# Cross-attention and soft mixture of experts: a new order of the attention steps, and key and value projections as three products of fp32r parts

## The chip, the cores and the metric

The kernel runs on one core of one Trainium2 chip. The metric is the device time of one execution, in microseconds (us). The granted clock of TensorE has two levels, 1.2 and 2.4 GHz; the profile gives it as a share of the higher.

## The reference, cut to what matters

```python
# B = 16 images, N = 100 queries, S = 361 context rows, D = 256, H = 16 heads of 16
q = layernorm(x) @ wq + bq
k = ctx @ wk + bk                      # 361 x 256 per image
v = ctx @ wv + bv
alpha = softmax(q k^T / 4 + mask)      # per head, 100 x 361
x = x + (alpha v) @ wo + bo
x = x + soft_moe(layernorm(x))         # 16 experts, not touched by the change
```

All inputs are fp32, and the result is compared in fp32.

## The kernel before, in words

`attention_phase` handles the 16 images one after another in a software pipeline, then a routing phase and an expert phase follow. The change touches only the attention phase.

The pipeline has steps t = -3 to 16. In step t each engine works for five images at once: keys and queries of image t+3, values of t+2, score maxima of t+1, probabilities and their product with the values for image t, and the output projection of t-1. Steps -3, -2 and -1 fill the pipeline and have a table of their own, `AT_FILL`. Keys exist up to step 12, values up to 13, maxima up to 14, probabilities up to 15. Steps 3 to 11 are three trips of a hardware loop over three steps; the others are written out.

A step has 24 slots. `AT` says in which slot each operation stands; a number of 24 or more means the slot minus 24 of the next step. All engines run the same slots in the same order, and each engine executes its own instructions strictly in that order, so the table sets what is queued behind what. Within a slot the order is that of the code in `part`.

The operations, with their keys in the table and lines in the profile:

- rows (L715, TensorE): scores of one head pair, 100 x 362, two matmuls, into `at_rows`; VectorE then reduces them to maxima (L496). There is one such bank pair, so rows r+1 waits for the reduction of r. Eight per step.
- maxT (L837), max_parts (L546, L548, VectorE), maxrow (L250): the maxima are transposed, split and sent by four small DMAs, two on the queue of SyncE and two on that of ScalarE, into rows of `qt`. rows 0 of the next step waits for max_parts, cols 0 for the DMAs.
- cols (L737, TensorE): transposed scores, four matmuls into `at_cols`; exp (L621, ScalarE) turns them into `p_f`. cols u+1 waits for exp u. Six per step.
- pv (L757): sixteen matmuls with 32 output columns each, that is with TensorE divided into four strips. Six per step.
- v (L785) and v_copy (L612): the value projection in three pieces of 121, 121 and 119 context rows, and its copy by ScalarE. k (L771), k_hi (L632, ScalarE), k_lo (L527, VectorE): the key projection in two halves c, and its split into fp32r parts. Both write the PSUM banks `at_proj`; so k waits for the copies of v, and the reverse.
- ln (L508, L511 VectorE; L391, L393 GpSimd: the reciprocal root `rstd`), xl (L639, L644 ScalarE), xlT (L804), xlT_out (L649), q (L812), q_hi (L655), q_lo (L534): normalised queries.
- sums (L664), oT (L819), att (L515, L519), attT (L824), attT_out (L669), y (L829), x1 (L540): output.
- `next_ctx` (L283) on SyncE loads the context of image b+4 (L261) after the values of b+1 are done.

In the last steps `stay_busy` (L723) puts matmuls on unread data between the others. `hidden_scales` (L1383) works out scales for the first two experts on VectorE; it waits for a round trip of DMAs that spreads maxima over the partitions (L1367, L1370).

Keys and values are fp32 matmuls. The profile shows each of them as two matmul instructions.

Of the kernel before, what the change touches and what calls it, by code (L numbers as in the profile page):

```python
# [1978 lines left out]
```

## Time and profile before

| | us |
|---|---|
| median of 3 runs | 1083.11 (1076.62 to 1083.24) |
| profiled execution | 1084.29 |
| its span, first to last instruction | 1082.5 |
| attention phase within it | 0 to 340.3 |
| mean granted clock | 0.982 |

The span and the trace are of one profiled execution; 1.8 us of it lie outside the span. Rows of a timeline merge neighbouring instructions of one kind: start, time from the first start to the last end, and the count. A matmul's duration holds its way through the array, so the distance between starts, not the duration, tells how long it keeps TensorE.

### The profile page before, as it was taken

To read this page: it belongs to the slowest core of one execution; us is meant where nothing else is said; L and a number is where in the kernel's file an instruction comes from. 1 tells how busy PE (TensorE), PEld (TensorE's weight loads), DVE (VectorE), ACT (ScalarE), POOL (GpSimd) and SP (SyncE) were. 2 spreads that over 40 slices of the span, in tenths; PEclk is the share of its full clock that TensorE was granted. 3 is DMA by queue.
4 is the path that set the end of the run, shared out by engine and by line. 5 is a ranking of instruction groups with operands and counts; after the bars stand their busy time and mean duration, and the time that the engine had idled before them with its cause. 6 is when DMAs were issued, how large, how long until landed. Compare 5 with 4: busy or idle time off the path is not lost.

```text
span 1082.5 us, 22394 instructions
## 1 busy us (share of the span) xinstructions
PE 1009.3 (93%) x7624; PEld 667.6 (62%) x7624; DVE 757.9 (70%) x1255; ACT 555.9 (51%) x1047; POOL 333.0 (31%) x448
## 2 busy tenths in 40 slices
PE   4789999999996898979999999999999999999996
PEld 3566777777653455646666666666666656666664
DVE  4555565656564677658878877787788788878754
ACT  1454455455432877853645554554635445545531
POOL 5121000000001333249434353353344343442220
PEclk8999999999997999999999999999999999999999
DMA  7978677676732444463335144352352351452122
GB/s 199 196 164 180 136 160 164 164 155 156 145 121 93 125 121 122 108 174 90 80 101 155 30 117 135 60 162 67 87 169 44 100 155 34 114 138 52 39 55 81
DMA packets 111456, 128.40 MB, mean 119 GB/s; under 512 B 37301, under 2 KB 98217, under 8 KB 111365
## 3 DMA queue, kind: packets, MB, share of 16 engines
q1 hardware_dynamic: 97340, 85.41, 35.1%
q0 software_dynamic: 11024, 40.61, 11.9%
q10 hardware_dynamic: 3000, 1.21, 0.6%
q8 instruction: 52, 0.85, 0.4%
q14 instruction: 40, 0.32, 0.1%
HBM read 80.22 MB, written 29.96 MB: 102 GB/s over the span
## 4 chain that ended last, share of the span: by engine, by line
PE 49%; DVE 2%; issue 2%; ACT 2%; DMA 1%; POOL 0%; SPq 0%; DVEq 0%; ACTq 0%; POOLq 0%
PE down L1878 14%; PE second L1233 13%; PE gate L1233 7%; PE up L1233 7%; PE mix L1826 4%; PE mix L1813 3%; ACT hid_h L1791 1%; DVE gate_sb L1677 1%; DVE hid_l L1689 1%; DMA eo_l<-eo 1%; PE mix L1810 0%; DVE x L1660 0%; DVE wd_l L1697 0%; ACT slot_h L1740 0%; PE mix L1823 0%
## 5 line engine op out<-in xcount | busy, mean ns | idle before, releaser
L496 DVE TENSOR_REDUCE head_max<-at_rows 100x2 f32<-100x722 f32 x124 | 112.9, 910 | 103.5 <-PE at_rows L715 103.5
L1878 PE MATMUL down<-wd_h,hid_h 128*128 128x256 f16 x512 | 139.8, 273 | 6.9 <-DVE hid_l L1689 5.8
L1878 PE MATMUL down<-wd_h,hid_l 128*128 128x256 f16 x512 | 139.5, 273 | 0.0
L1878 PE MATMUL down<-wd_l,hid_h 128*128 128x256 f16 x512 | 139.5, 272 | 0.0
L1791 ACT ACTIVATE hid_h<-gate_sb,hid_scale 128x512 f16<-128x512 f32 x128 | 92.1, 720 | 80.6 <-DVE gate_sb L1677 79.9
L1689 DVE SCALAR_TENSOR_TENSOR hid_l<-gate_sb,hid_scale,hid_h 128x512 f16<-128x512 f32 x128 | 108.2, 845 | 35.8 <-ACT hid_h L1791 34.3
L621 ACT ACTIVATE p_f<-at_cols 121x800 f32<-121x800 f32 (+1 forms) x96 | 80.5, 838 | 85.7 <-PE at_cols L737 50.8
L1592 POOL TENSOR_TENSOR eo_l<-eo_l,eo_h 128x512 fp32r<-128x512 f32 x60 | 80.6, 1344 | 130.4 <-ACT eo_h L1748 130.2
L1770 ACT ACTIVATE gate_sb<-gate,bgu,un_gate 128x512 f32<-128x512 f32 x63 | 48.6, 771 | 137.1 <-PE gate L1233 137.0
L715 PE MATMUL at_rows<-kt,qt 100*100 100x362 f32 x248 | 75.6, 386 | 7.1 <-DMA qt<-q_parts 3.6
L1233 PE MATMUL second<-slot_h,wgu_h 128*128 128x512 f16 x256 | 76.7, 381 | 1.7 <-DVE gate_sb L1677 1.7
L1233 PE MATMUL second<-slot_l,wgu_h 128*128 128x512 f16 x256 | 76.5, 381 | 0.0
L1233 PE MATMUL second<-slot_h,wgu_l 128*128 128x512 f16 x256 | 76.2, 379 | 0.0
L1711 DVE SCALAR_TENSOR_TENSOR eo<-down,un_down,bd 128x512 f32<-128x512 f32 x64 | 47.2, 747 | 36.7 <-PE down L1878 36.0
L391 POOL TENSOR_SCALAR var_eps<-mv 100x1 f32<-100x1 f32 x16 | 3.6, 224 | 212.9 <-DVE mv L511 212.9
L1149 PE MATMUL second<-seT,rt_xnT 128*100 128x512 f32 x128 | 63.4, 641 | 2.8 <-ACT rt_xnT L1093 1.7
L737 PE MATMUL at_cols<-qt,kt 104*121 104x200 f32 (+1 forms) x384 | 61.1, 282 | 3.3 <-DMA qt<-max_p 2.6
L1878 PEld LDWEIGHTS down<-wd_h,hid_h 128*128 128x128 f16 x512 | 49.9, 97 | 22.6 <-issue 15.4
L1651 DVE TENSOR_TENSOR slot_l<-mix,slot_h 128x512 f16<-128x512 f32 x60 | 41.4, 689 | 26.4 <-ACT slot_h L1740 26.2
L1660 DVE SCALAR_TENSOR_TENSOR x<-mix,rz,x 100x256 f32<-100x256 f32 x128 | 55.8, 478 | 3.2 <-PE mix L1823 3.0
L737 PEld LDWEIGHTS at_cols<-qt,kt 104*121 104x121 f32 (+1 forms) x384 | 50.1, 184 | 11.8 <-ACT p_f L621 6.9
L1677 DVE SCALAR_TENSOR_TENSOR gate_sb<-up,bu_s,gate_sb 128x512 f32<-128x512 f32 x63 | 47.0, 746 | 14.5 <-PE up L1233 14.2
(207 smaller groups left out, 2429.7 us busy)
## 6 DMA issues: line engine op xcount, KB each, us to landing
eo_l<-eo SPq DMA_DIRECT2D x128, 128.0 KB, 2.4
k_parts<-kq_n SPq DMA_DIRECT2D x16, 724.0 KB, 4.3
kt<-k_parts SPq DMA_DIRECT2D x32, 362.0 KB
wgu<-in_Wg POOLq DMA_DIRECT2D x16, 512.0 KB, 4.5
wgu<-in_Wu POOLq DMA_DIRECT2D x16, 512.0 KB, 5.7
wd<-in_Wd POOLq DMA_DIRECT2D x16, 512.0 KB, 6.0
combine<-combT SPq DMA_DIRECT2D x16, 400.0 KB, 3.6
dispatch<-dispT SPq DMA_DIRECT2D x16, 400.0 KB
```

The lines of the kernel that those rows point to most:

```text
L496: nc.vector.tensor_reduce(head_max[:, :, r], bank[0:N, :, 0:S], AX.X, ALU.max).then_inc(max_ready, 1)
L621: nc.scalar.activation(p_f[u][0:kn].rearrange("k (g e) n -> k g (e n)", g=2), cols_ps[0:kn, :, 0:4 * N], ACT.Exp, scale=1.0 / SCALE_INV).t ...
L715: mm = nc.tensor.matmul(bank[0:N, c, 0:SW], q[0:ROWS_A, c, r, :], k[0:ROWS_A, r, :], start=True, stop=True)
L737: mm = nc.tensor.matmul(out, kt[t % NBUF][0:ROWS_B, r, j * KC:j * KC + kn], qt[t % NBUF][0:ROWS_B, :, r, :], start=True, stop=True)
L1149: mm = nc.tensor.matmul(logits[0:N, g, :], xnT[:, c, :], seT[:, c, g * BANK:(g + 1) * BANK], start=(c == 0), stop=(c == 1))
L1233: mm = nc.tensor.matmul(bank, wt[:, kc, i, c * P:(c + 1) * P], st[:, kc, e, :, :].rearrange("p b s -> p (b s)"), start=(k == 0), stop=(k = ...
L1592: nc.gpsimd.tensor_tensor(eo_l[h][:, bs], eo_l[h][:, bs].bitcast(F32), eo_h[h][:, bs].bitcast(F32), ALU.subtract).then_inc(eol_ready, 1)
L1660: add = nc.vector.scalar_tensor_tensor(acc[:, b, :], mix_ps[1 - r % 2][0:N, i * D:(i + 1) * D], rz[:, b:b + 1], acc[:, b, :], ALU.mult, AL ...
L1677: nc.vector.scalar_tensor_tensor(gate[c % 2][:], up_ps[c % 2], keep["bu_s"][:, bass.ds(FC * ex + c, 1)], gate[c % 2][:], ALU.add, ALU.mult ...
L1689: nc.vector.scalar_tensor_tensor(hid_l[:, c, :], gate[c % 2][:], keep["hid_scale"][:, bass.ds(ex, 1)], hid_h[:, c, :], ALU.mult, ALU.subtr ...
L1791: nc.scalar.activation(hid_h[:, c, :], gate[c % 2][:], ACT.Copy, scale=keep["hid_scale"][:, bass.ds(ex, 1)]).then_inc(hidh_ready, 1)
L1878: mm = nc.tensor.matmul(down_ps[t // 2][:, t % 2, :], ht[:, c, t * P:(t + 1) * P], wt[:, c, :], start=(c == 0 and k == 0), stop=(c == FC - ...
```

## The change

The slots of the steady table move: the probabilities' cols and exp one to three slots earlier, pv in pairs in the same step, the output (sums to x1) to early slots, and xlT and q next to each other. The context and the weights `wk`, `wv` are split into a high part in fp32r (ScalarE) and a remainder (GpSimd), and each fp32 product becomes three fp32r products. `stay_busy` before pv stands only before every second one, and `hidden_scales` moves from step 15 to step 16. Two buffers per context image are added.

```diff
 AT = {
-    "cols": (6, 8, 10, 12, 14, 18), "exp": (6, 8, 10, 12, 14, 18), "pv": (10, 12, 16, 19, 26, 28),
+    "cols": (5, 7, 9, 11, 13, 15), "exp": (5, 7, 9, 11, 13, 15), "pv": (10, 10, 14, 14, 18, 18),
...
-    "sums": 5, "oT": 8, "att": 9, "attT": 11, "attT_out": 12, "y": 18, "x1": 26,
-    "k": (8, 16), "k_hi": (8, 16), "k_lo": (9, 18), "ln": 0, "xl": 1, "xlT": 12, "xlT_out": 12,
-    "q": 14, "q_hi": 14, "q_lo": 15,
+    "sums": 0, "oT": 3, "att": 4, "attT": 6, "attT_out": 6, "y": 18, "x1": 19,
+    "k": (8, 16), "k_hi": (8, 16), "k_lo": (9, 18), "ctx_hi": 0, "ln": 0, "xl": 1, "xlT": 11, "xlT_out": 11,
+    "q": 12, "q_hi": 12, "q_lo": 14,
 }
...
+        def context_low(p, par):
+            pool.wait_ge(ctx_hi, p + 1)
+            pool.sem_inc(waited, 1)
+            nc.gpsimd.tensor_tensor(cx_l[par][:, :, 0:S], cx[par][:], cx_h[par][:, :, 0:S].bitcast(F32), ALU.subtract).then_inc(ctx_lo, 1)
...
+        for n in range(2):
+            pool.wait_ge(w_hi, n + 1)
+            nc.gpsimd.tensor_tensor(w["kv"[n]][:], w_in_full["kv"[n]], w_h["kv"[n]][:].bitcast(F32), ALU.subtract).then_inc(w_lo, 1)
+            if n == 0:
+                context_low(0, 0)
...
             if keys:
+                if t > -3:
+                    context_low(p, (t + 3) % NBUF)
                 norm_rstd()
...
+                if t == B and s == AT["att"] + 1:
                     hidden_scales(nc, dve, keep, 0)
...
+        act.wait_ge(w_in["k"], 16)
+        nc.scalar.activation(w_h["k"][:], w_in_full["k"], ACT.Copy).then_inc(w_hi, 1)
...
+                if s == tab["ctx_hi"]:
+                    turn = trip + (t + 3) // NBUF
+                    act.wait_ge(ctx_in[(t + 3) % NBUF], 16 * (turn + 1))
+                    if t >= 0:
+                        act.wait_ge(v_done, 2 * b + 2)
+                    act.sem_inc(waited, 1)
+                    nc.scalar.activation(cx_h[(t + 3) % NBUF][:, :, 0:S], cx[(t + 3) % NBUF][:], ACT.Copy).then_inc(ctx_hi, 1)
+                    if t == -3:
+                        act.wait_ge(w_in["v"], 16)
+                        nc.scalar.activation(w_h["v"][:], w_in_full["v"], ACT.Copy).then_inc(w_hi, 1)
...
-                if t >= B - 2:
+                if t >= B - 2 and i % 2 == 0:
                     stay_busy(1)
...
-                    turn = trip + (t + 3) // NBUF
-                    pe.wait_ge(ctx_in[(t + 3) % NBUF], 16 * (turn + 1))
+                    pe.wait_ge(ctx_lo, p + 1)
...
                 for kc in range(2):
-                    mm = nc.tensor.matmul(k_ps[c], w["k"][:, kc, c * P:(c + 1) * P], cx_p[:, kc, :], start=(kc == 0), stop=(kc == 1))
+                    for i, (wt, xt) in enumerate(((w_h["k"], high), (w_h["k"], low), (w["k"], high))):
+                        mm = nc.tensor.matmul(k_ps[c], wt[:, kc, c * P:(c + 1) * P], xt[:, kc, :], start=(kc == 0 and i == 0), stop=(kc == 1 and i == 2))
...
                 for kc in range(2):
-                    mm = nc.tensor.matmul(v_ps[g][0:kn, j - V_GROUPS[g][0], :], cx_n[:, kc, j * KC:j * KC + kn], w["v"][:, kc, :],
-                                          start=(kc == 0), stop=(kc == 1))
+                    for i, (xt, wt) in enumerate(((high, w_h["v"]), (high, w["v"]), (low, w_h["v"]))):
+                        mm = nc.tensor.matmul(v_ps[g][0:kn, j - V_GROUPS[g][0], :], xt[:, kc, j * KC:j * KC + kn], wt[:, kc, :],
+                                              start=(kc == 0 and i == 0), stop=(kc == 1 and i == 2))
```

Three places show how the order moves. The lines of the changed kernel are its own: L748 is rows, L770 cols, L790 pv, L805 keys, L839 xlT, L847 q, L820 values, L872 maxT.

On TensorE in the second half of a step, before, from the attT transposes on (L824), two pv groups, a rows and a cols stand around xlT (L804), and q (L812) comes four entries after it:

```order
L824 MATMUL at_out<-ident,att 128x100 x2
L737 MATMUL at_cols<-qt,kt 121x200 x4
L804 MATMUL at_proj<-ident,xl 128x100 x2
L757 MATMUL at_out<-p_f,v_s 32x100 x8
L715 MATMUL at_rows<-kt,qt 100x362 x2
L737 MATMUL at_cols<-qt,kt 119x200 x4
L812 MATMUL at_proj<-xlT,w_q 128x100 x4
L715 MATMUL at_rows<-kt,qt 100x362 x2
L771 MATMUL at_proj<-cx,w_k 128x361 x2
L757 MATMUL at_out<-p_f,v_s 32x100 x8
```

And the same place in the changed kernel:

```order
L790 MATMUL at_out<-p_f,v_s 32x100 x16
L748 MATMUL at_rows<-kt,qt 100x362 x2
L770 MATMUL at_cols<-qt,kt 121x200 x4
L839 MATMUL at_proj<-ident,xl 128x100 x2
L847 MATMUL at_proj<-xlT,w_q 128x100 x4
L748 MATMUL at_rows<-kt,qt 100x362 x2
L770 MATMUL at_cols<-qt,kt 119x200 x4
L790 MATMUL at_out<-p_f,v_s 32x100 x16
L748 MATMUL at_rows<-kt,qt 100x362 x2
```

Two pv groups have become one of twice the length, and nothing is left between xlT and q.

On ScalarE around the start of a step, before, from the maxima's DMAs (L250) on:

```order
L250 DMA qt<-max_p 1x8x100 x2
L621 ACTIVATE p_f<-at_cols 119x800
L639 ACTIVATE x_dev<-xn,mv 100x256
L644 ACTIVATE xl<-x_dev,rstd 100x256
L612 ACTIVATE v_s<-at_proj 121x32x16
L664 ACTIVATE sums<-at_out 128x400
L621 ACTIVATE p_f<-at_cols 121x800
```

And in the changed kernel, where L255 are these DMAs, L653 ctx_hi, L697 sums, L672 and L677 xl, L635 v_copy and L644 exp:

```order
L255 DMA qt<-max_p 1x8x100 x2
L653 ACTIVATE cx_h<-cx 128x2x361
L697 ACTIVATE sums<-at_out 128x400
L672 ACTIVATE x_dev<-xn,mv 100x256
L677 ACTIVATE xl<-x_dev,rstd 100x256
L635 ACTIVATE v_s<-at_proj 121x32x16
L644 ACTIVATE p_f<-at_cols 121x800
```

The copy of the context's high part stands ahead of xl, v_copy and the first exp of the step.

On GpSimd at the start of the program, before (L381 is the fill of `unread`, L391 and L393 the reciprocal root, L400 fills of `kt`, L403 and L405 the slot embeddings' root):

```order
L381 MEMSET unread 128x512
L391 ISA
L391 TENSOR_SCALAR var_eps<-mv 100x1
L393 TENSOR_TENSOR rstd<-var_eps,neg_half 100x1
L400 MEMSET kt 32x2896 x2
L403 TENSOR_SCALAR slot_ve<-slot_mv 128x8
L405 TENSOR_TENSOR slot_rs<-slot_ve,neg_half 128x8
L391 TENSOR_SCALAR var_eps<-mv 100x1
```

And in the changed kernel:

```order
L396 TENSOR_TENSOR w_k<-p_f,w_h_k 128x512
L385 TENSOR_TENSOR cx_l<-cx,cx_h 128x2x361
L396 TENSOR_TENSOR w_v<-p_f,w_h_v 128x512
L399 MEMSET unread 128x512
L409 TENSOR_SCALAR var_eps<-mv 100x1
L411 TENSOR_TENSOR rstd<-var_eps,neg_half 100x1
L420 MEMSET kt 32x2896 x2
L423 TENSOR_SCALAR slot_ve<-slot_mv 128x8
L425 TENSOR_TENSOR slot_rs<-slot_ve,neg_half 128x8
L385 TENSOR_TENSOR cx_l<-cx,cx_h 128x2x361
L409 TENSOR_SCALAR var_eps<-mv 100x1
```

Three subtractions stand ahead of the first reciprocal root, and one ahead of each later one.

## Rows read from the trace of the kernel before

**Rows 1.** The page, busy time of each engine over the span.

```profile
PE 1009.3 (93%) x7624; PEld 667.6 (62%) x7624; DVE 757.9 (70%) x1255; ACT 555.9 (51%) x1047; POOL 333.0 (31%) x448
```

**Rows 2.** From one rows 0 to the next, steps 0, 2, 6, 13: length, busy, clock.

```profile
50.40:69.00 18.60, 15.71 (x138) 11.88 (x136) 9.02 (x14) 9.10 (x17) 2.35 (x1) 0.93 0.78 178
...
86.30:106.00 19.70, 17.20 (x182) 12.63 (x178) 10.60 (x20) 10.99 (x20) 3.91 (x5) 1.00 0.86 166
...
177.50:194.90 17.40, 17.23 (x182) 12.64 (x178) 10.62 (x20) 9.25 (x17) 0.79 (x2) 1.00 0.72 161
...
282.00:297.50 15.50, 14.51 (x166) 10.15 (x159) 8.71 (x13) 6.41 (x10) 0.00 (x0) 1.00 0.68 146
```

**Rows 3.** Timeline of TensorE in step 6: start, us, instruction.

```profile
178.02 0.55 PE L757 MATMUL at_out<-p_f,v_s 119*32 119x100 f32 x16
178.50 1.13 PE L785 MATMUL at_proj<-w_v,cx 128*121 128x256 f32 x4
...
183.89 1.40 PE L771 MATMUL at_proj<-cx,w_k 128*128 128x361 f32 x4
185.12 0.60 PE L819 MATMUL at_out<-ident,sums 128*100 128x128 f32 x4
...
189.92 1.05 PE L812 MATMUL at_proj<-xlT,w_q 128*128 128x100 f32 x8
...
191.14 1.38 PE L771 MATMUL at_proj<-cx,w_k 128*128 128x361 f32 x4
...
192.93 0.25 PE L837 MATMUL at_rows<-ident,head_max 100*16 100x100 f32 x1
```

**Rows 4.** Timeline of TensorE in the expert phase: fp32r products of 256 columns.

```profile
592.22 0.28 PE L1826 MATMUL mix<-eo_h,comb_h 128*100 128x256 f32 x1
592.33 0.28 PE L1826 MATMUL mix<-eo_h,comb_l 128*100 128x256 f32 x1
```

**Rows 5.** Groups by line over the span: busy us, mean ns of one.

```profile
L1791 ACT ACTIVATE hid_h<-gate_sb,hid_scale 128x512 f16<-128x512 f32 x128 | 92.1, 720 | 80.6 <-DVE gate_sb L1677 79.9
...
L1592 POOL TENSOR_TENSOR eo_l<-eo_l,eo_h 128x512 fp32r<-128x512 f32 x60 | 80.6, 1344 | 130.4 <-ACT eo_h L1748 130.2
...
L1309 ACT ACTIVATE wgu_h<-wgu,w_scale 128x2048 f16<-128x2048 f32 x16 | 31.9, 1996 | 28.5 <-DVE w_scale L1405 28.5
...
L374 POOL TENSOR_TENSOR x<-xn,bo_v 100x1024 f32<-100x1024 f32 x4 | 9.5, 2366 | 6.4 <-DMA xn<-in_x 6.4
```

**Rows 6.** Timeline around step 6, ScalarE and its queue, GpSimd.

```profile
189.27 0.33 ACT L649 ACTIVATE xlT<-at_proj 128x200 f32<-128x200 f32 x1
...
190.12 0.84 ACT L621 ACTIVATE p_f<-at_cols 119x800 f32<-119x800 f32 x1 [0.30 <-PE at_cols L737]
...
193.88 1.31 ACTq L250 DMA_DIRECT2D qt<-max_p  x2
...
195.25 0.22 POOL L391 TENSOR_SCALAR var_eps<-mv 100x1 f32<-100x1 f32 x1 [16.50 <-DVE mv L511]
195.55 0.57 POOL L393 TENSOR_TENSOR rstd<-var_eps,neg_half 100x1 f32<-100x1 f32 x1
```

**Rows 7.** Timeline of the start, ScalarE.

```profile
13.03 0.20 ACT L599 ACTIVATE warm<-neg_half 128x1 f32<-128x1 f32 x1
...
16.26 1.01 ACT L632 ACTIVATE kq_n<-at_proj,bk 128x361 fp32r<-128x361 f32 x2 [2.10 <-DMA bq<-in_bq]
```

**Rows 8.** Timeline of step 0; its last row gives the DMA's time to landing.

```profile
52.47 0.38 SPq L261 DMA_DIRECT2D cx<-in_ctxT  x1
...
59.30 0.58 PE L737 MATMUL at_cols<-qt,kt 104*121 104x200 f32 x4
...
cx<-in_ctxT SPq DMA_DIRECT2D x1, 361.0 KB, 5.6
```

**Rows 9.** Timeline of the attention phase's end.

```profile
334.92 1.06 PE L819 MATMUL at_out<-ident,sums 128*100 128x128 f32 x4 [4.98 <-DVE x L540]
...
339.88 0.43 DVE L540 TENSOR_TENSOR x<-at_out,x 100x256 f32<-100x256 f32 x1 [3.15 <-PE at_out L829]
```

More of the change, by code:

```diff
@@ L54 @@
     "v": (0, 1, 2), "v_copy": (1, 2),
-    "ln": 0, "xl": 3, "k": (3, 4), "k_hi": (4, 6), "k_lo": (5, 7), "xlT": 5, "xlT_out": 6,
+    "ctx_hi": 0, "ln": 0, "xl": 3, "k": (3, 4), "k_hi": (4, 6), "k_lo": (5, 7), "xlT": 5, "xlT_out": 6,
     "q": 7, "q_hi": 8, "q_lo": 9,
@@ L139, in attention_phase @@
     out_ps = [psum(f"at_out{i}", [P, BANK]) for i in range(2)]
-    k_ps = [t[:, 0:S] for t in proj]
+    k_ps = [t[:, 0:SW] for t in proj]
     xlT_ps = proj[0][:, 0:2 * N].rearrange("p (c n) -> p c n", c=2)
@@ L149, in attention_phase @@
     o_ps = out_ps[0][:, 0:GROUPS * N].rearrange("p (g n) -> p g n", g=GROUPS)
-    w = {n: sb(f"w_{n}", [P, 2, D], F32) for n in ("q", "k", "v", "o")}
+    w = {n: sb(f"w_{n}", [P, 2, D], F32R if n in ("k", "v") else F32) for n in ("q", "k", "v", "o")}
     bq, bk = sb("bq", [P, 2], F32), sb("bk", [P, 2], F32)
@@ L154, in attention_phase @@
     bo, bo_v = sb("bo", [N, D], F32), sb("bo_v", [N, D], F32)
-    p_f = [sb(f"p_f{i}", [KC, HH, N], F32) for i in range(NHALF)]
+    p_f = [sb(f"p_f{i}", [P, HH, N], F32) for i in range(NHALF)]
+    w_in_full = {n: p_f[3 + i][:].rearrange("p h n -> p (h n)")[:, 0:2 * D].rearrange("p (c n) -> p c n", c=2) for i, n in enumerate(("k", "v"))}
     mask_in, mask_f = (p_f[i][0:B].rearrange("b h n -> b (h n)")[:, 0:S] for i in range(2))
@@ L159, in attention_phase @@
     cx = [sb(f"cx{i}", [P, 2, S], F32) for i in range(NBUF)]
+    cx_l = [sb(f"cx_l{i}", [P, 2, SW], F32R) for i in range(NBUF)]
+    cx_h = [sb(f"cx_h{i}", [P, 2, SW], F32R) for i in range(NBUF)]
+    w_h = {n: sb(f"w_h_{n}", [P, 2, D], F32R) for n in ("k", "v")}
     stats, mv, rstd = sb("stats", [N, 6], F32), sb("mv", [N, 2], F32), sb("rstd", [N, 1], F32)
@@ L203, in attention_phase @@
     sums_ready, oT_done = sem("sums_ready"), sem("oT_done")
+    ctx_hi, ctx_lo, w_hi, w_lo = sem("ctx_hi"), sem("ctx_lo"), sem("w_hi"), sem("w_lo")
     s_done, max_ready, maxT_done, max_parts = sem("s_done"), sem("max_ready"), sem("maxT_done"), sem("max_parts")
@@ L375, in residual @@
                                     ALU.add).then_inc(base_ready, 1)
+        def context_low(p, par):
+            pool.wait_ge(ctx_hi, p + 1)
+            pool.sem_inc(waited, 1)
+            nc.gpsimd.tensor_tensor(cx_l[par][:, :, 0:S], cx[par][:], cx_h[par][:, :, 0:S].bitcast(F32), ALU.subtract).then_inc(ctx_lo, 1)
         pool.memset(one_rows, 1.0).then_inc(qt_zero, 1)
+        for i in range(NBUF):
+            pool.memset(cx_l[i][:, :, S:SW].bitcast(F32), 0.0).then_inc(unread_set, 1)
+            pool.memset(cx_h[i][:, :, S:SW].bitcast(F32), 0.0).then_inc(unread_set, 1)
         for i in range(NBUF):
@@ L631, in part @@
                             act.wait_ge(k_stored, 16 * p)
-                        nc.scalar.activation(kq_n[:, c, 0, 0:S], k_ps[c], ACT.Identity, bias=bk[:, c:c + 1]).then_inc(k_hi, 1)
+                        nc.scalar.activation(kq_n[:, c, 0, 0:S], k_ps[c][:, 0:S], ACT.Identity, bias=bk[:, c:c + 1]).then_inc(k_hi, 1)
                 if s == tab["xl"]:
```

15 lines of the change are left out of this document (8 added, 7 removed).

## The prediction

> **What bounds the kernel now.** I read the page first: TensorE is busy 93% of the span [rows 1]. That is an average over three phases, and the change touches one, the attention phase, some 340 of 1082.5 us. So next come the stretches from one rows 0 to the next. An undisturbed step takes 17.4 us, TensorE is busy 17.23 of it, VectorE 10.62, ScalarE 9.25 and GpSimd 0.79 [rows 2]. Then the timeline of TensorE, where the distance between starts is read, not the duration. Keys take 185.12 - 183.89 = 1.23 us for four instructions, 0.303 each [rows 3]. Two fp32r matmuls of 362 columns (rows 5, between q and k) take what is left of 191.14 - 189.92 after eight q instructions: these start (1.05 - 0.275) / 7 = 0.11 apart (0.275 is the median duration of one), so 0.88, and the two take 0.34, 0.17 each at most [rows 3]. Values follow each other at 0.215, a group of four at 0.86, and 0.1 more behind a pv group. One pv group holds TensorE for 178.50 - 178.02 = 0.48 us and 0.09 ahead of it [rows 3]; 0.30 of that is its sixteen starts, the rest a pause on either side of the change between strips and the whole array. Adding up such distances, 16.9 of the 17.4 us are occupied and 0.5 is waiting. TensorE bounds a step, by an order that has other work wherever it would wait.
>
> **The change, part by part: TensorE's work.** Keys: twelve fp32r instructions of 362 columns at 0.163 in place of eight at 0.303, 1.96 for 2.45 us, saves 0.5 a step. Values: eighteen at 0.118 (starts of fp32r products of 256 columns lie 0.11 to 0.12 apart [rows 4]) in place of twelve at 0.215, and no longer behind a pv group: 2.13 for 2.8 us, saves 0.7. Pv in pairs: three entries and exits less, 0.6, and some 0.1 of exposed weight loads. So 15.0 us of work instead of 16.9. Were the waits to stay at 0.5, a step would take 15.5.
>
> **The waits that the order adds.** First, q directly behind xlT. Between them ScalarE must copy xlT, and in its order exp 3 comes first, which waits for cols 3, the entry before xlT on TensorE. From the start of cols 3: 0.63 until exp can start, its copy follows 0.74 later (a ScalarE instruction starts that much after an exp of 0.84 [rows 6]), the copy 0.33 [rows 6], the handover 0.05: q starts 1.75 after cols 3, and TensorE has work (cols 0.42, xlT 0.18) for 0.60. It stands 1.15 us, in every step with keys; before, pv, rows and cols lay there.
>
> Second, the head of the step on ScalarE. Count from the start of maxT, called M. The maxima are ready and the DMAs issue at M + 0.95 and hold ScalarE for 1.31 [rows 3, 6]. Only then ctx_hi: 722 elements at a rate between 512 in 0.720 and 2048 in 1.996 [rows 5], so 0.87. GpSimd takes over after 0.22 (VectorE to GpSimd takes that at the same place) and subtracts 722 elements: 512 took 1.344, 1024 took 2.366 [rows 5]; the line through them gives 1.76, the slower rate 1.90, the faster 1.67. I take 1.76. Then the reciprocal root, 0.87 from start to end [rows 6], for which xl waits: 0.13 and 0.51. Then v_copy (0.50 until the next can start, 0.1 of overlap), exp 0 0.84, 0.06 to cols 1. The sum: M + 8.0 for cols 1. What TensorE has until then: y, two pv, rows 0, values, rows 1, oT, values, rows 2, cols 0, attT, values, rows 3, with the reductions of VectorE between, ends at M + 7.3. So it stands 0.7 us. After cols 1 the rest of the step up to the next M is 0.5 + 0.98 + 0.33 + 0.42 + 0.94 + 0.41 + 0.42 + 0.18 + 1.15 + 0.98 + 0.33 + 0.42 + 0.94 + 0.41 + 0.42 + 0.98 = 9.8 (cols 1, keys, rows, cols, pv pair, rows, cols, xlT, the wait, q, rows, cols, pv pair, rows, cols, keys). **A step takes 17.8 us where it took 17.4**: the waits eat the 1.9 us and a little more. Eleven steps (1 and 3 to 12) are like this, +4.4 us. Step 2 took 19.7 [rows 2], since rows 0 of the next waited for a DMA behind two loads of norm vectors, and I leave it. If the chain were hidden, 17.2 and -2; with 1.90 on GpSimd and 0.3 of further handovers 18.3 and +10.
>
> The row of GpSimd is 2.3 to 2.6 ns per element. The Trainium skill, "GPSIMD Engine Reference", section "Elementwise — side-by-side cycle accounting", gives about 2.6 cycles for two inputs, which at its 1.2 GHz would be an estimate of 1.56 us here and a step of 17.6; its section "Engine selection" says to give such work to VectorE, which has seven of 17.4 us free here. That rule speaks against the remainder on GpSimd, and the trace shows the order of size that it states.
>
> **The start.** ScalarE is free at 13.23 [rows 7]. Now come the high parts of wk (0.72), of the context (0.87) and of wv; on GpSimd 1.34 for wk from 14.0 on, 1.76 for the context, 1.34 for wv, 0.5 for `unread`, 0.9 for the root: 19.9, and xl 20.4. k_hi stands behind xl in ScalarE's order and started at 16.26, waiting for a bias [rows 7]. So +4.2 us, and everything up to rows 0 of step 0 is a chain behind it. In step -2 GpSimd has 5 us of fills and the slot embeddings first, which adds 1 us on its own image and is caught up. I take +4.3, from 3 to 6.
>
> **Step 0.** The context of image 3 is issued at 52.47 and lands 5.6 later, at 58.1 [rows 8]; before, only keys at slot 8 needed it. Now ctx_hi needs it in slot 0 on ScalarE, with xl, v_copy and exp 0 behind it. With the shift it lands at 62.4. From there 0.87 + 0.22 + 1.76 + 0.87 + 0.13 + 0.51 + 0.50 + 0.84 + 0.06 = 5.8 to cols 1, 68.2; before 59.30 [rows 8] plus the shift, 63.6. That is +4.6, and the rest of the step +1.1 (10.8 for 9.7). In such a gap of some 5 us the clock may fall: in step 0 it already was 0.93 [rows 2]; I add 0.3 and in all +6, from 3 to 8.
>
> **The end.** Steps 13 to 15 have no keys, no ctx_hi and no such waits. By the same adding up step 13 takes 14.9 for 15.5 [rows 2], step 14 1.9 less (three fewer matmuls of `stay_busy`, pairs), step 15 waits for the maxima's DMAs and gains nothing: -2.3 us. Then `hidden_scales`: oT waited 4.98 us for an x1 that stood behind it on VectorE [rows 9]. x1 of image 14 now comes before it. From sums to the last x1 it was 339.88 - 329.94, 9.9 and its own 0.4; now 0.5 + 0.75 + 0.75 + 3.0 (the scales, now behind att) + 0.4 = 5.4: -4.9. If the clock stays up through the end, up to 3 more; I take -7.5 in all, from -5 to -11.
>
> **The sum.** 4.3 + 6 + 4.4 - 7.5 = +7.2 us, on the profiled execution 1084.3 and 1091.5. The median of the runs is 1.2 below that execution, so 1090.3; **I say 1090**.
>
> **Rivals.** *TensorE's work decides* (faster): if xlT's copy and the context chain find cover that I don't see, a step takes 15.5 to 16.5. For it speaks that TensorE is occupied 97% of a step now; against it that in-order ScalarE has no other entry between cols 3 and q. 11 x -1.5 + 4.3 + 4 - 7.5 = -16: 1067. *The GpSimd chain decides more than I think* (slower): this is one mechanism, ctx_hi, remainder, root, xl, v_copy, exp 0, with its place at the head of the step; it costs time from M + 7.3 on, so each 0.1 us of it is paid. 
> **How the numbers follow.** The forecast (1074 to 1094) has 0.50, the faster rival 0.15, the slower 0.32, the last 0.03. The range 1074 to 1101 holds the forecast and most of the slower rival, and leaves out the faster one below 1074 and the last: 0.8. 1%, 10.8 us, is about what a measurement of this kernel can tell from none; from the cases, faster 0.15, same 0.50, slower 0.35.
>
> **What would show it.** In the profile after: steps near 17.8 with TensorE less busy; q released by ScalarE's copy of xlT with a gap of 1.1 us; xl on ScalarE waiting for GpSimd's root; context remainder 1.7 to 1.9 us; in step 0 a wait for the context's DMA ahead of ctx_hi; starts of keys 0.163 and of values 0.118 apart; the 4.98 us wait gone at the end. I would be wrong if steps were at 16.5 or less, if ctx_hi came ahead of the maxima's DMAs in time, or if the start were hidden by the bias loads.

## The result, and the profile after

| | before | after |
|---|---|---|
| median (lowest to highest), us | 1082.22 (1076.62 to 1087.46), 18 runs | 1090.67 (1082.48 to 1099.15), 18 runs |
| ratio, 95% interval | 1 | 1.0081 [1.0061, 1.0101] |
| profiled execution, us (span) | 1084.3 (1082.5) | 1082.48 (1080.7) |
| mean granted clock of that execution | 0.982 | 0.984 |

The change costs 0.8%: the medians are 8.45 us apart. The profiled execution of after is the fastest of its 18 runs, so its rows show where time goes within a phase, while the size of the whole is the median's. A second profile of the same kernel (after_again, below) lies nearer to the median. One run of after, 1099.15, is over 1.5% above the fastest, counts as a slow one and is not in the ratio.

The page of after. Each line has busy time, share of the span and count; the second line shown is the granted clock in 40 slices of 27 us.

```profile
PE 981.6 (91%) x7772; PEld 685.2 (63%) x7778; DVE 760.9 (70%) x1255; ACT 568.4 (53%) x1065; POOL 363.8 (34%) x472
...
PEclk9879999999999999999999999999999999999999
```

Against [rows 1], TensorE has 28 us less to do, GpSimd 31 us more, and the span is only 1.8 us shorter. The next view is the stretches from one rows 0 to the next (length, then busy time of TensorE, its weight loads, VectorE, ScalarE and GpSimd, then clock): step 0, step 2, step 7 and step 13 of after. (Counted from step 0 at 50.40, the stretch at 177.50 in [rows 2], called step 6 ahead, is step 7; no number hangs on the name.)

```profile
52.32:78.08 25.76, 19.10 (x181) 16.93 (x179) 8.93 (x14) 10.64 (x19) 4.68 (x4) 0.73 0.57 128
96.34:113.73 17.39, 15.76 (x192) 13.73 (x188) 10.75 (x20) 9.95 (x18) 4.69 (x4) 1.00 0.83 175
184.58:202.07 17.49, 15.77 (x191) 13.72 (x188) 10.69 (x20) 9.95 (x18) 2.36 (x3) 1.00 0.73 160
290.20:305.54 15.34, 12.94 (x170) 10.72 (x166) 8.81 (x13) 6.78 (x11) 0.00 (x0) 1.00 0.69 148
```

In step 7 TensorE is busy 15.77 us where it was 17.23 [rows 2], and the step is 0.1 us longer: 1.5 us of saved work have become waiting. The timeline of TensorE in that step shows where:

```profile
186.16 0.57 PE L748 MATMUL at_rows<-kt,qt 100*100 100x362 f32 x2 [0.29 <-DVE head_max L516]
...
190.42 0.67 PE L770 MATMUL at_cols<-qt,kt 104*121 104x200 f32 x4 [0.45 <-ACT p_f L644]
190.93 0.35 PE L805 MATMUL at_proj<-cx_h,w_h_k 128*128 128x362 f32 x1
191.11 0.33 PE L805 MATMUL at_proj<-cx_l,w_h_k 128*128 128x362 f32 x1
191.28 0.33 PE L805 MATMUL at_proj<-cx_h,w_k 128*128 128x362 f32 x1
...
195.74 1.14 PE L847 MATMUL at_proj<-xlT,w_q 128*128 128x100 f32 x8 [0.98 <-ACT xlT L682]
```

Two waits are those of the prediction: cols 1 behind exp 0, 0.45 us, and q behind ScalarE's copy of xlT, 0.98 us. The third, 0.29 us for VectorE's reduction, is short. Read the starts of the keys, not their durations: 0.17 apart, against 0.303 for the instructions that they replace [rows 3]. The values start 0.118 apart (185.11, 185.23, 185.35).

The chain that ends at exp 0, on ScalarE, its queue and GpSimd, in the same step:

```profile
183.66 1.32 ACTq L255 DMA_DIRECT2D qt<-max_p  x2
185.13 0.81 ACT L653 ACTIVATE cx_h<-cx 128x722 fp32r<-128x722 f32 x1 [1.66 <-issue]
...
188.65 0.51 ACT L677 ACTIVATE xl<-x_dev,rstd 100x256 f32<-100x256 f32 x1 [1.92 <-issue]
...
189.54 0.83 ACT L644 ACTIVATE p_f<-at_cols 121x800 f32<-121x800 f32 x1
...
186.12 1.60 POOL L385 TENSOR_TENSOR cx_l<-cx,cx_h 128x722 fp32r<-128x722 f32 x1 [15.14 <-ACT cx_h L653]
187.69 0.22 POOL L409 TENSOR_SCALAR var_eps<-mv 100x1 f32<-100x1 f32 x1
187.99 0.57 POOL L411 TENSOR_TENSOR rstd<-var_eps,neg_half 100x1 f32<-100x1 f32 x1
```

ScalarE's xl shows 1.92 us of waiting put down to "issue", since the releaser, GpSimd's root, is not matched to it. The times tell it: the root ends at 187.99 + 0.57 = 188.56, and xl starts 0.09 later.

Step 0, ScalarE and TensorE. Here [rows 8] had cols 1 at 59.30. The first fence is ScalarE, the second TensorE.

```profile
60.10 0.81 ACT L653 ACTIVATE cx_h<-cx 128x722 fp32r<-128x722 f32 x1 [6.47 <-DMA cx<-in_ctxT]
```

```profile
59.47 1.13 PE L770 MATMUL at_cols<-qt,kt 104*121 104x200 f32 x4 [2.80 <-DMA qt<-max_p]
...
65.40 1.13 PE L770 MATMUL at_cols<-qt,kt 104*121 104x200 f32 x4 [2.88 <-ACT p_f L644]
```

The context was issued at 53.85 on SP's queue and ctx_hi starts at 60.10. Cols 1 comes 5.3 us behind that.

The start, on ScalarE and GpSimd. It answers to [rows 7]:

```profile
11.25 0.20 ACT L620 ACTIVATE warm<-neg_half 128x1 f32<-128x1 f32 x1
...
17.66 0.51 ACT L677 ACTIVATE xl<-x_dev,rstd 100x256 f32<-100x256 f32 x1 [4.08 <-POOL rstd L411]
18.08 0.55 ACT L665 ACTIVATE kq_n<-at_proj,bk 128x361 fp32r<-128x361 f32 x1
```

And the end, which answers to [rows 9]:

```profile
339.06 0.64 PE L854 MATMUL at_out<-ident,sums 128*100 128x128 f32 x4 [0.62 <-ACT sums L697]
...
344.69 3.68 PE L1184 MATMUL second<-seT,rt_xnT 128*100 128x512 f32 x8 [0.43 <-ACT rt_xnT L1128]
```

oT waits 0.62 us where it waited 4.98, and the last x1 starts at 343.15.

### The profile page after: what moved, and what is told of

Its sections match the earlier page's. It is cut to its first block, busy times and chain, and to the rows that moved or that the text cites. A ratio compares the mean times of both kernels' runs of the same rounds, so it can differ in the third digit from the quotient of the medians.

```text
span 1080.7 us, 22774 instructions
## 1 busy us (share of the span) xinstructions
PE 981.6 (91%) x7772; PEld 685.2 (63%) x7778; DVE 760.9 (70%) x1255; ACT 568.4 (53%) x1065; POOL 363.8 (34%) x472
## 4 chain that ended last, share of the span: by engine, by line
PE 50%; DVE 2%; ACT 2%; issue 2%; DMA 0%; DVEq 0%; SPq 0%; ACTq 0%
PE down L1913 15%; PE second L1268 14%; PE gate L1268 7%; PE up L1268 7%; PE mix L1861 4%; PE mix L1848 3%; ACT hid_h L1826 1%; DVE gate_sb L1712 1%; DVE hid_l L1724 1%; PE mix L1858 0%; PE mix L1845 0%; ACT gate_sb L1805 0%; ACT slot_h L1775 0%; DVE wd_l L1732 0%; DMA eo_l<-eo 0%
## 5 line engine op out<-in xcount | busy, mean ns | idle before, releaser
L644 ACT ACTIVATE p_f<-at_cols 121x800 f32<-121x800 f32 (+1 forms) x96 | 80.3, 837 | 54.7 <-PE at_cols L770 53.7
L385 POOL TENSOR_TENSOR cx_l<-cx,cx_h 128x722 fp32r<-128x722 f32 x16 | 25.7, 1608 | 201.9 <-ACT cx_h L653 201.9
L748 PE MATMUL at_rows<-kt,qt 100*100 100x362 f32 x248 | 69.8, 363 | 8.2 <-DVE head_max L516 7.4
L770 PE MATMUL at_cols<-qt,kt 104*121 104x200 f32 (+1 forms) x384 | 59.7, 279 | 12.8 <-ACT p_f L644 10.0
L770 PEld LDWEIGHTS at_cols<-qt,kt 104*121 104x121 f32 (+1 forms) x384 | 53.9, 188 | 21.2 <-ACT p_f L644 16.6
L1184 PE MATMUL second<-seT,rt_xnT 128*100 128x512 f32 x128 | 60.2, 614 | 2.6 <-ACT rt_xnT L1128 1.5
L1686 DVE TENSOR_TENSOR slot_l<-mix,slot_h 128x512 f16<-128x512 f32 x60 | 41.4, 690 | 26.8 <-ACT slot_h L1775 26.7
```

The costliest lines, as they stand in the source:

```text
L644: nc.scalar.activation(p_f[u][0:kn].rearrange("k (g e) n -> k g (e n)", g=2), cols_ps[0:kn, :, 0:4 * N], ACT.Exp, scale=1.0 / SCALE_INV).t ...
L748: mm = nc.tensor.matmul(bank[0:N, c, 0:SW], q[0:ROWS_A, c, r, :], k[0:ROWS_A, r, :], start=True, stop=True)
L770: mm = nc.tensor.matmul(out, kt[t % NBUF][0:ROWS_B, r, j * KC:j * KC + kn], qt[t % NBUF][0:ROWS_B, :, r, :], start=True, stop=True)
L1184: mm = nc.tensor.matmul(logits[0:N, g, :], xnT[:, c, :], seT[:, c, g * BANK:(g + 1) * BANK], start=(c == 0), stop=(c == 1))
```

## The experiments

Each was timed beside the kernel before on the same chip, and ratios are to that kernel. There were three chips: one for order_only, parts_only, split_late and q_later (median of before there 1082.37), one for low_twice, hidden_back, after_again and the kernel called both (1081.94), one for root_first, both_again and both_hidden (1080.52). Across chips it is the ratios that compare. The last column is step 7 or, in low_twice, the range of steps 2 to 8. "Chain" below means maxima DMAs, ctx_hi, remainder, root, xl, exp 0, cols 1.

| kernel | what it is | median us (runs) | ratio [95%] | an undisturbed step, us |
|---|---|---|---|---|
| after | | 1090.67 (18) | 1.0081 [1.0061, 1.0101] | 17.5 |
| after_again | the same | 1089.15 (8) | 1.0060 [1.0035, 1.0086] | 17.5 |
| order_only | new order, old products | 1079.12 (12) | 0.9973 [0.9944, 1.0001] | 17.45 |
| parts_only | old order, new products | 1101.59 (6) | 1.0189 [1.0134, 1.0244] | 18.0 |
| low_twice | remainder twice | 1133.94 (6) | 1.0487 [1.0462, 1.0513] | 19.7 to 20.9 |
| root_first | root ahead of remainder | 1081.40 (12) | 1.0003 [0.9977, 1.0028] | 16.8 |
| split_late | that, and ctx_hi at slot 2 | 1075.91 (12) | 0.9942 [0.9913, 0.9971] | 16.8 |
| q_later | q one slot later | 1084.12 (12) | 1.0016 [0.9990, 1.0041] | 16.9 |
| both | split_late and q_later | 1069.29 (6) | 0.9888 [0.9859, 0.9917] | 16.25 |
| both_again | the same | 1070.56 (9) | 0.9922 [0.9896, 0.9947] | 16.25 |
| both_hidden | both, scales back | 1071.39 (9) | 0.9917 [0.9889, 0.9945] | 16.25 |
| hidden_back | after, scales back | 1090.49 (6) | 1.0088 [1.0062, 1.0113] | 17.5 |

### Which half costs: order_only and parts_only

order_only is the kernel before with the new table, every second `stay_busy` and the late `hidden_scales`:

```diff
-AT = {...}   # the old table
+AT = {...}   # the new one; keys and values stay fp32 products
-                if t >= B - 2:
+                if t >= B - 2 and i % 2 == 0:
                     stay_busy(1)
+                if t == B and s == AT["att"] + 1:
                     hidden_scales(nc, dve, keep, 0)
```

> The kernel before with the new table, the thinner stay_busy and the moved hidden_scales, but fp32 projections. Theory of the prediction (the waits eat what TensorE saves): q still stands right behind xlT, so a step keeps that wait of 1.1 us and saves pairs of pv and exposed weight loads, 17.2 to 17.4 us a step; no context chain, no later start, no wait in step 0; the end gives 5 to 8 us back. Together -8, 1074 us, clock as before. Rival, the clock decides: the new order lets TensorE stand more often, the mean granted clock goes from 0.982 to about 0.973 as in most runs of the changed kernel, and the time is at or above 1082 us although the steps are no longer.

It measured 1079.12, 3 us under before where 8 were expected, and the interval reaches up to 1. In its step 7 TensorE is busy 0.9 us less than in [rows 2] and the step is not shorter:

```profile
176.86:194.31 17.45, 16.33 (x181) 13.14 (x178) 10.68 (x20) 9.58 (x17) 0.79 (x2) 1.00 0.73 160
```

Its list of waits has the one of q, here at the load of its weights, in each of four steps (columns: waiting engine and line, releaser, us in total, times, longest):

```profile
PEld at_proj L813 <- ACT xlT L650: 4.8, 4, 1.2
```

So the wait of q belongs to the order, not to the products, and it eats what the pairs of pv save. The gain is at the end: step 13 starts 0.2 us earlier than before, the last x1 ends 5.3 us earlier, and its oT waits 0.62 us too.

parts_only is the changed kernel with the old table (ctx_hi added at slot 0), the old `stay_busy` and the old place of `hidden_scales`.

> The changed kernel with the table of before (ctx_hi at slot 0), the stay_busy of before and hidden_scales in step 15: the fp32r parts alone. Theory of the prediction: the context chain at the head of the step delays cols 1 by some 1.1 us against 0.5 saved on keys behind it, 17.9 to 18.1 us a step; start +2, step 0 +4 to +6, the wait of 5 us at the end stays. Together +13, 1095 us. Rival, TensorE's work decides: 1.0 to 1.2 us a step less, 16.3 us, 1070 us.

It measured 1101.59, 19 us over before, where 13 were expected. The parts alone lengthen the start (rows 0 of step 0 at 56.12, +5.7 for an expected +2), step 0 (26.7 us, +8.1 for an expected +4 to +6) and steps 1 to 12 (+4.7 together), although TensorE has 0.75 us less to do in a step than in [rows 2]:

```profile
192.62:210.62 18.00, 16.48 (x192) 13.23 (x188) 10.60 (x20) 9.84 (x18) 2.36 (x3) 1.00 0.70 155
```

The chain's wait alone is there, and it is three times that of after:

```profile
199.54 0.67 PE L769 MATMUL at_cols<-qt,kt 104*121 104x200 f32 x4 [1.36 <-ACT p_f L643]
```

In the old order exp 5 still stands between the maxima's DMAs and ctx_hi. Order and parts don't add: -3.3 and +19.2 would be +15.9, and together they are +8.5.

### The chain, made longer: low_twice

```diff
                 if t > -3:
+                    pool.wait_ge(ctx_hi, p + 1)
+                    nc.gpsimd.tensor_tensor(cx_l[...], cx[...], cx_h[...], ALU.subtract).then_inc(twice, 1)
+                    pool.wait_ge(twice, p)
                     context_low(p, (t + 3) % NBUF)
```

> GpSimd's subtraction of the context's remainder is done twice in each step, ahead of the reciprocal root, at 1.60 us each; nothing else changes. Theory (the chain maxima DMA, ctx_hi, remainder, root, xl, exp 0 stands on the path that sets the step): each step from 1 to 13 grows by near 1.6 us, less what slack it has where the second copy moves past, step 0 and the start by up to 1.6 us each: 12 x 1.3 to 1.6 = 16 to 19, with the ends 1106 to 1113 us. Rival (a step is set by TensorE's own work and the wait of q alone, the chain has cover): under 5 us in all, 1091 to 1096 us.

It measured 1133.94, 43 us over after (by the ratios 44): the theory's direction, at over twice its size. Two steps of its trace, steps 6 and 7, first the windows, then cols 1 and the keys of the step at 210.12, then GpSimd:

```profile
190.38:210.12 19.74, 15.83 (x188) 13.61 (x188) 10.89 (x20) 9.94 (x18) 3.96 (x4) 1.00 0.62 142
210.12:230.84 20.72, 17.29 (x191) 15.15 (x187) 10.67 (x20) 9.94 (x18) 3.97 (x4) 0.92 0.59 135
```

```profile
217.66 0.72 PE L774 MATMUL at_cols<-qt,kt 104*121 104x200 f32 x4 [2.15 <-ACT p_f L648]
218.18 0.55 PE L809 MATMUL at_proj<-cx_h,w_h_k 128*128 128x362 f32 x1
218.53 0.50 PE L809 MATMUL at_proj<-cx_l,w_h_k 128*128 128x362 f32 x1
218.83 0.51 PE L809 MATMUL at_proj<-cx_h,w_k 128*128 128x362 f32 x1
```

```profile
211.55 1.60 POOL L417 TENSOR_TENSOR cx_l<-cx,cx_h 128x722 fp32r<-128x722 f32 x1 [15.04 <-ACT cx_h L657]
213.36 1.61 POOL L386 TENSOR_TENSOR cx_l<-cx,cx_h 128x722 fp32r<-128x722 f32 x1 [0.20 <-POOL cx_l L417]
```

The second subtraction costs its 1.60 us and 0.20 from the first's end to its own start, 1.8, and the wait of cols 1 grows from 0.45 to 2.15 in step 7. Step 6 is the one of steps 1 to 12 in which the clock stayed at 1.00. It took 19.74, and the same step of after took 18.02:

```profile
166.56:184.58 18.02, 15.82 (x188) 13.59 (x188) 10.90 (x20) 9.94 (x18) 2.36 (x3) 1.00 0.69 155
```

That is 1.7 us, so all of the longer chain is paid. The other steps from 1 to 12 have a mean clock of 0.92 (one has 0.85) and are 3.2 to 3.3 us longer than the same steps of after (that one 4.5). So the clock adds 1.5 us to a step, nearly as much as the chain, and TensorE's busy time shows it: 17.29 us in step 7 for 15.83 in step 6. Behind the wait of 2.15 us the keys start 0.30 apart, at 1.2 GHz, where they were 0.17 apart; behind the wait of 2.35 us in step 6 they did not. I had priced the expectation without the clock.

### The chain, taken out: root_first and split_late

root_first moves one call for the steps from 0 on:

```diff
-                if t > -3:
+                if -3 < t < 0:
                     context_low(p, (t + 3) % NBUF)
                 norm_rstd()
+                if t >= 0:
+                    context_low(p, (t + 3) % NBUF)
```

split_late does this, and moves ctx_hi behind xl:

```diff
-    ..., "ctx_hi": 0, "ln": 0, "xl": 1, ...
+    ..., "ctx_hi": 2, "ln": 0, "xl": 1, ...
```

> The changed kernel with ctx_hi at slot 2 instead of 0 (behind xl on ScalarE) and, from step 0 on, the subtraction behind the reciprocal root on GpSimd. Theory of the prediction: xl, and through it v_copy and exp 0, no longer wait for the subtraction; cols 1 waits no more; 17.1 to 17.3 us a step and about 3 us less in step 0: -8 to -11 against the changed kernel, 1080 to 1083 us. Rival, the chain is not what delays cols 1: steps stay at 17.5 to 18.0, less than 3 us gained.

> The changed kernel with one half of the edit of split_late: from step 0 on GpSimd computes the reciprocal root before the context's remainder; ctx_hi stays at slot 0 ahead of it on ScalarE. Theory (what stretched the step was the remainder of 1.60 us and its handover of 0.2 ahead of the root, and with it xl and exp 0): most of the 14.8 us of split_late comes back, 1078 to 1082 us, steps near 16.9 us, xl no longer waiting 1.9 us; only step 0's wait of ctx_hi for its context stays, up to 4 us. Rival (ctx_hi's own 0.81 us and its wait at the head of the step are what counts): 1086 to 1091 us, steps of 17.3 us or more.

split_late measured 1075.91, 15 us under after and better than expected; root_first 1081.40, 9 us under after (by the ratios 8), as expected. The step is the same 16.8 us in both, and cols 1 does not wait in step 7 of either, so GpSimd's remainder ahead of the root, and not ctx_hi on ScalarE, is what stretched the steps. Between the two kernels the ratios leave 0.6%, 6 to 7 us, which the steps don't hold. In the profiles they differ in step 0 (22.9 against 21.4 us) and in the tail, where root_first's profile has a clock of 0.90 from 326 to 360 us and split_late's 1.00 from 325 to 360; how much of the difference is the position of ctx_hi and how much the clock is open. Step 0 of split_late on ScalarE:

```profile
54.33 0.50 ACT L674 ACTIVATE x_dev<-xn,mv 100x256 f32<-100x256 f32 x1
54.86 0.51 ACT L679 ACTIVATE xl<-x_dev,rstd 100x256 f32<-100x256 f32 x1
61.12 0.81 ACT L655 ACTIVATE cx_h<-cx 128x722 fp32r<-128x722 f32 x1 [5.75 <-DMA cx<-in_ctxT]
61.83 0.58 ACT L637 ACTIVATE v_s<-at_proj 121x512 f32<-121x512 f32 x1
62.31 0.83 ACT L646 ACTIVATE p_f<-at_cols 121x800 f32<-121x800 f32 x1
```

xl no longer stands behind the context, and from ctx_hi to exp 0 it is 1.2 us, where it was 64.52 - 60.10 = 4.4.

### The other wait: q_later, and both

```diff
-    "q": 12, "q_hi": 12, "q_lo": 14,
+    "q": 13, "q_hi": 13, "q_lo": 14,
```

> The changed kernel with q and q_hi at slot 13 instead of 12, so that rows 6 and cols 4 stand between xlT and q on TensorE. Theory of the prediction: the wait of 1.0 to 1.2 us ahead of q goes, a wait of 0.5 to 0.6 us for VectorE's reduction ahead of rows 6 takes its place: -0.5 us a step, 1085 us. Rival, VectorE's chain of reductions was late anyway: no change, 1090 us. Rival, the clock decides: the time follows the mean granted clock and not the steps.

It measured 1084.12, 6.5 us under after, as expected. All waits of TensorE in its step 7:

```profile
186.62 0.57 PE L748 MATMUL at_rows<-kt,qt 100*100 100x362 f32 x2 [0.29 <-DVE head_max L516]
190.87 0.67 PE L770 MATMUL at_cols<-qt,kt 104*121 104x200 f32 x4 [0.45 <-ACT p_f L644]
195.63 0.57 PE L748 MATMUL at_rows<-kt,qt 100*100 100x362 f32 x2 [0.41 <-DVE head_max L516]
```

The wait of q, 0.98, is gone, and 0.41 at the rows that came to stand there has taken its place: VectorE's reduction frees their bank. Hence 0.55 us a step and not 1.

> This kernel is the changed one with two entries moved: ctx_hi to slot 2 and, from step 0 on, GpSimd's remainder behind the reciprocal root; and q with q_hi one slot later. Theory (the chain ahead of cols 1 and the wait of q behind xlT each stretch the step, TensorE's own work does not): alone they took off 14.8 and 6.5 us of the median. If they are independent the median is 1090.7 - 21.3 = 1069.4. Rival (after the first of them a step already stands at 16.85 us, near TensorE's own work, so the second has little left to take): 1072 to 1076 us, steps of 16.6 to 16.85 us. With the clock lost at the start, as in the run with q later, up to 6 us more on either.

> The version with both edits again, on this chip, as the base of both_hidden and to have its ratio twice: 1067 to 1071 us, 0.986 to 0.992 of the kernel before. Rival (the first ratio was luck of six runs): 0.993 or more.

The two together measured 1069.29 and on another chip 1070.56, 1.1% and 0.8% under the kernel before (0.9922 is at the edge of what was expected of the second), and by the ratios 21 and 17 us under after. In the steps the edits add exactly: 17.49 less 0.69 (split_late) and 0.55 (q_later) is 16.25. It is the fastest version; split_late alone is under the kernel before too. A step of it:

```profile
174.69:190.94 16.25, 15.54 (x191) 13.74 (x187) 10.77 (x20) 10.29 (x18) 2.40 (x3) 1.00 0.77 172
```

TensorE is busy 15.54 of 16.25. The 0.71 us that are left are these two waits, both on VectorE:

```profile
176.27 0.57 PE L750 MATMUL at_rows<-kt,qt 100*100 100x362 f32 x2 [0.30 <-DVE head_max L518]
...
184.59 0.57 PE L750 MATMUL at_rows<-kt,qt 100*100 100x362 f32 x2 [0.41 <-DVE head_max L518]
```

### The end: hidden_back and both_hidden

```diff
-                if t == B and s == AT["att"] + 1:
-                    hidden_scales(nc, dve, keep, 0)
+                    hidden_scales(nc, dve, keep, 0)
```

> hidden_scales goes back to the last step, ahead of VectorE's part of the tail; all else is as in the changed kernel. Theory (in the step after the last it hides behind ScalarE's and TensorE's tail, before it stood ahead of x1 and oT): the stretch from the last pv to the layer norm's end grows by the 4.4 to 4.9 us that the oT wait was, the median is 1095 to 1096 us. Rival (the tail is shorter for another reason, the new order's last slots): within 1.5 us of 1090.7.

> The version with both edits and hidden_scales back in the last step. The trace of hidden_back showed the stretch from the last sums to the end of the last x1 as 7.5 us instead of 4.6. Theory (that 2.9 us is real and the median of hidden_back only hid it): 1.5 to 4 us over both_again, 1071 to 1073 us, with the reduction waiting for the landing of all_hidden ahead of VectorE's x1. Rival (it is hidden): within 1 us of both_again.

Medians: 1090.49 for hidden_back, where after_again on the same chip had 1089.15; 1071.39 for both_hidden, where both_again had 1070.56. In both pairs it is about 1 us, less than these runs can tell from nothing, so by the times it is the rival of both expectations that came out. The traces show more. VectorE and oT in hidden_back:

```profile
340.31 1.06 DVE L1430 TENSOR_REDUCE top<-all_hidden 128x4 f32<-128x516 f32 x1 [3.59 <-DMA all_hidden<-hidden_maxima]
...
343.65 0.61 PE L853 MATMUL at_out<-ident,sums 128*100 128x128 f32 x4 [3.24 <-DVE x L560]
```

The reduction waits for a landing, with x1 of the image before and the last att behind it. From the last sums to the last x1 it is 348.00 - 340.48 = 7.5 us, in after_again 343.12 - 338.48 = 4.6. The other pair repeats it: 7.5 in both_hidden, 4.6 in both_again. In the kernel before it was 339.88 - 330.01 = 9.9. So of the 5.3 us that the tail became shorter, 2.9 go with the place of `hidden_scales` in these traces. Some of that is clock: y takes 2.03 us in hidden_back and in before, 1.28 in after_again. The other 2.4 lie between hidden_back and before, which differ in order, products and clock at once; no run parts them. Either way 4.4 was too much to expect. Why the 2.9 us hardly show in the medians is open.

### The spread: after_again

> The changed kernel as it is, to have a profile of an ordinary execution, since the one on record is the fastest of its runs. Theory (the attention's steps take the same time in every execution and the spread comes from stretches at the lower clock at the start or in the expert part): a median of 1088 to 1092 us, rows-to-rows distances as on record within 0.3 us, and where the span is 5 to 10 us longer, slices with a granted clock under 9 that the first profile does not have. Rival (the step itself varies): distances that differ by over 0.3 us at the same granted clock.

Median 1089.15, its profiled execution 1086.18. The undisturbed steps repeat within 0.1 us (step 7 is 17.48 and was 17.49), so the step does not vary. Step 1 starts 1.7 us later, at 79.81, after a stretch at a lower clock. The steps from 13 on give that back, since there the first profile has a clock of 0.90 from 305.5 to 323 us and this one 1.00: the last x1 ends at 343.54 in one and 343.57 in the other. Then the routing product of eight matmuls takes 5.68 us for 3.68, and 1.5 us of the 3.7 between the spans lie further behind. Windows of after_again and of after (the clock is the third number from the end):

```profile
20.00:78.20 58.20, 42.37 (x266) 37.55 (x265) 28.30 (x63) 21.73 (x46) 15.90 (x14) 0.74 0.73 160
340.00:350.00 10.00, 7.37 (x16) 2.97 (x16) 5.31 (x19) 0.67 (x2) 4.93 (x10) 0.66 0.33 90
```

```profile
20.00:78.10 58.10, 41.97 (x303) 37.16 (x303) 29.30 (x66) 23.10 (x48) 16.56 (x15) 0.79 0.73 163
340.00:350.00 10.00, 5.97 (x21) 2.67 (x22) 5.76 (x21) 1.79 (x3) 4.90 (x10) 1.00 0.28 95
```

Before had 0.91 from 20.00 to 69.00, the same part of the program. Its routing product ran at the lower clock too, 6.02 us, so against before only the first of these two stretches is new.

## Why the prediction was right

1090 was forecast and 1090.67 measured; the case of most chance, waits in place of work, is what happened, and the experiments show both waits. That the number came out to 0.7 us is in part luck. The sum was +7.2 us and the medians differ by 8.45, but its terms don't add up to that in either profile, each against the profile of before:

| term | forecast, us | after | after_again |
|---|---|---|---|
| start, rows 0 of step 0 | +4.3 | 52.32 against 50.4: +1.9 | 54.56: +4.2 |
| step 0 | +6 | 25.76 against 18.6: +7.2 | 25.25: +6.7 |
| steps 1 to 12 | +4.4 | 212.1 against 213.0: -0.9 | 212.1: -0.9 |
| step 13 to the end of the last x1 | -7.2 | 53.4 against 58.3: -4.9 | 51.7: -6.6 |
| clock in the routing product | -0.3 | 3.68 us against 6.02: -2.3 | 5.68: -0.3 |
| sum | +7.2 | +1.0 | +3.1 |

The last x1 ends 3.2 us later in both profiles than in that of before. The rest of the 8.45 lies in no term of the sum. Part of it is which executions were profiled: that of before is 2.1 us above its median, those of after are 8.2 and 3.0 below theirs. The clock, below, is what the runs show of it.

**TensorE's work.** Keys at 0.163 and values at 0.118 were forecast; the trace has 0.167 and 0.118. The rival of two passes is out. The work saved shows as busy time: 17.23 to 15.77.

**The wait of q** was 1.15 by the sum and is 0.98. It comes from the order: order_only has it, and q_later removes it.

**The chain.** Its count begins at M, the start of maxT, 182.71 in this step, and the maxima's DMAs issue at 183.66, M + 0.95 as forecast. ctx_hi was forecast for M + 2.26 and came at M + 2.4, the remainder took 1.60 and not 1.76, cols 1 came at M + 7.7 and not M + 8.0. TensorE ran out of work at 189.97, M + 7.3 as forecast. So 0.45 us of wait for 0.7. low_twice, root_first and split_late show that this chain sets the step: lengthened by 1.8 it costs 1.7 where the clock stays up, taken out it gives 0.7 a step. The rest of the step, 9.8 from cols 1 to the next M, came out at 200.20 - 190.42 = 9.8.

**A step** was to go from 17.4 to 17.8. Over the nine undisturbed steps 4 to 12 it went from 17.45 (157.0 us for nine) to 17.64 (158.7), so +0.2. Of these, steps 6 and 9, each the first of a trip of the hardware loop, take 18.0; the others take 17.5 to 17.65. Step 1 took 1.0 more, and steps 2 and 3 took 3.6 less, since the wait of 2.33 us for a DMA behind step 2 and a stretch at the lower clock in step 3 (0.91) did not come back. I had left step 2 as it was. The eleven steps that the sum counts give +1.4 for +4.4, and this term is the one that both profiles miss.

**The start** was +4.3 in the sum and +1.9 in after. ScalarE was free at 11.45 and not 13.23, since the last DMA issue ahead of `warm` took 1.7 us for 3.1, and each remainder of weights took 1.27 us. xl started at 17.66, not 20.4, and k_hi at 18.08. The chain through GpSimd to xl was as told, with 4.08 us of wait. In after_again k_hi is earlier still, at 17.52, and yet rows 0 of step 0 comes at 54.56: the clock is 0.72 from 20 us up to it, in after 0.84. So its +4.2 agrees with the forecast for another reason than the forecast's.

**Step 0** went as told and cost 1.2 more: ctx_hi waited 6.47 us for its context, cols 1 came at 65.40. The wait of 2.80 us at cols 0 is old (it was 2.64 in the kernel before), the 2.88 at cols 1 is new, and behind them TensorE ran at 1.2 GHz for more of the step: the mean clock is 0.73 where [rows 2] has 0.93. From cols 1 to the end of the step it took 12.7 us for a forecast of 10.8. I had given the clock 0.3 us.

**The end** gave 4.9 for 7.2. From step 13 to the last sums I gave 2.3 us; it went from 48.0 to 48.3 in after, with the clock at 0.90 for 17 us of it, and to 46.6 in after_again, at 1.00: 1.4 of the 2.3. The wait of oT fell from 4.98 to 0.62. The last sums to the end of the last x1 went from 10.3 us to 343.57 - 338.51 = 5.1, so 5.2 for a forecast of 4.9.

**The clock** is the term that I priced at nothing over all, 0.3 us in step 0 and as much the other way at the end. The first profiles of the two are only 0.7 us apart at the end of the routing product (348.37 and 347.65); the medians are 8.45 apart. Every run lists its mean granted clock: 0.9746 over 17 runs of after, 0.9798 over the 29 of before that were timed beside the first experiments. A straight line through time against clock gives at a clock of 0.98 some 1085.9 us for after and 1082.2 for before. So about 4 of the 8.45 us go with a lower clock, and about 4 are left at the same clock, where the sum said 7.2. That is a relation between runs and not an experiment; where an ordinary run of after loses clock against before is shown only for after_again, 0.74 over the start and step 0. Whether the waits of step 0 cause it stays open: filling them with work was not tried.

**GpSimd.** The remainder took 1.60 us for 722 elements, 2.2 ns each. By the Trainium skill, "GPSIMD Engine Reference", section "Elementwise — side-by-side cycle accounting", the estimate was 1.56, and the trace agrees to 3%. What its section "Engine selection" says, to give such work to VectorE, was not tried; in root_first, where it stays on GpSimd behind the root, step 7 has no wait that leads back to it.

The faster rival (TensorE's work decides) is false for this kernel and nearly true for both: 16.25 us a step with 15.54 busy, within the 15.5 to 16.5 that it gave, and 1069.29 and 1070.56 us for its 1067. Its lower end, 15.5, no run reached; what is left in both are waits for VectorE's reductions.

## What to carry to other kernels

Work taken off the engine that bounds a step is worth only what the next chain leaves: here 1.5 us of TensorE's step were saved and nearly all of it went into two waits (0.45 and 0.98), each set by what stood ahead in another engine's order. Before adding an operation to an engine that is nearly idle, look at what stands behind it in its order: 1.6 us on GpSimd, busy 0.8 of 17.4 us, cost 0.7 us a step ahead of a root that others waited for, and behind it no wait that the trace shows. Between a transpose and the product that reads its copy, leave entries of work for the time that the copy's engine needs, with what stands ahead of the copy in its order counted in: with none between xlT and q TensorE stood 0.98 us, with a rows and a cols between them 0.41, and that for VectorE. And a forecast that comes out right as a sum still has to be held against its terms: here one profile gave +1.0 and the other +3.1 for +7.2.
